# Mixture-of-experts block after cross-attention: expert tiles run in two phases, routing of the last batches placed between tiles

## The reference

```python
x = x + xattn(_layernorm(x), ctx_1024, mask, mask, Wq, Wkv, Wc)      # 16 heads of 8, softmax over 128 keys
logits = xf @ router_w.T                       # xf = layernorm(x), 4096 tokens, 8 experts
top_vals, top_idx = top_k(logits, 2); probs = softmax(top_vals)
for e in range(8):
    w = sum(where(top_idx == e, probs, 0))
    h = gelu(xf @ w1[e].T + b1[e])             # 128 -> 512
    out += w[:, None] * (h @ w2[e].T + b2[e])  # 512 -> 128
x = x + out
```

## Time and profile before

| | us |
|---|---|
| median of 3 runs | 504.89 (502.22 to 506.77) |
| the profiled execution, own time | 509.84 |
| its span | 507.7 |
| TensorE busy | 368.2 (73%) |
| VectorE busy | 281.1 (55%) |
| ScalarE busy | 230.5 (45%) |
| GpSimd busy | 224.6 (44%) |
| mean granted clock of TensorE | 0.84 |

### The profile page before, as it was taken

One profiled execution on the slowest core, in us unless ns is written; L12 is line 12 of the kernel. 1 busy time (PEld: TensorE's weight loads), 2 busy tenths in 40 slices (PEclk: granted clock), 3 DMA queues, 4 the chain that ended last, 5 costly groups with the idle time before them and its releaser, 6 DMA issues.

```text
span 507.7 us, 12389 instructions
## 1 busy us (share of the span) xinstructions
PE 368.2 (73%) x3715; PEld 285.6 (56%) x3715; DVE 281.1 (55%) x883; ACT 230.5 (45%) x536; POOL 224.6 (44%) x316
## 2 busy tenths in 40 slices
PE   2548889797979878585596400899898999998900
PEld 1133556464646545363364300899797998887900
DVE  7167998779666766554343762344343444443426
ACT  1314677667364654433354100466454665554500
POOL 7883422312370724334607471255453555444520
PEclk9999998879786798775767555899998999999965
DMA  4795345635242332010101023555565655565358
GB/s 125 176 254 156 98 119 108 151 85 139 79 123 77 103 96 71 26 40 29 43 5 38 23 68 96 162 168 182 158 181 161 180 174 171 159 184 167 95 163 334
DMA packets 57119, 63.00 MB, mean 124 GB/s; under 512 B 14109, under 2 KB 40116, under 8 KB 56896
## 3 DMA queue, kind: packets, MB, share of 16 engines
q1 hardware_dynamic: 51584, 53.22, 37.9%
q0 software_dynamic: 4320, 8.47, 4.9%
q10 hardware_dynamic: 1152, 0.53, 0.4%
HBM read 37.65 MB, written 11.88 MB: 98 GB/s over the span
## 4 chain that ended last, share of the span: by engine, by line
PE 40%; DVE 14%; SPq 13%; issue 9%; DMA 9%; another core or an unknown queue 7%; ACT 5%; ACTq 0%; POOLq 0%; POOL 0%; DVEq 0%
PE smax L1117 9%; PE sexp L1126 8%; DVE shift L1186 5%; PE tail L950 5%; PE smax L906 5%; DMA stacks<-dispatch_d 4%; PE feed L985 3%; SPq L409 2%; SPq L493 2%; SPq L486 2%; SPq L494 2%; PE feed L897 2%; ACT probs L752 2%; SPq L487 2%
## 5 line engine op out<-in xcount | busy, mean ns | idle before, releaser
L1186 DVE TENSOR_REDUCE shift<-smax 128x4 f32<-128x512 f32 x128 | 85.9, 683 | 68.3 <-PE smax L906 41.2
L752 ACT ACTIVATE probs<-sexp 128x512 f32<-128x512 f32 x128 | 73.9, 593 | 41.6 <-PE sexp L914 29.5
L632 POOL DMA_INDIRECT dispatch_d<-rows_out,row_i x64 | 63.0, 984 | 64.1 <-DVE row_i L1338 47.5
L681 POOL DMA_INDIRECT result_d<-y_out,stacks x71 | 70.8, 997 | 38.4 <-issue 36.4
L1557 DVE TENSOR_TENSOR probs<-smax,b_cols 128x512 f32<-128x512 f32 x71 | 49.1, 691 | 68.3 <-PE smax L1117 66.4
L1117 PE MATMUL smax<-probs,w_ring 128*128 128x128 f32 x568 | 81.7, 289 | 3.8 <-ACT probs L857 1.7
L1126 PE MATMUL sexp<-w_sb,probs 128*128 x568 | 79.0, 283 | 1.0 <-ACT probs L861 1.0
L1117 PEld LDWEIGHTS smax<-probs,w_ring 128*128 128x128 f32 x568 | 71.7, 198 | 11.6 <-issue 10.3
L906 PE MATMUL smax<-stacks 64*128 64x128 bf16 x512 | 59.5, 250 | 23.6 <-DVE shift L1186 10.5
L1126 PEld LDWEIGHTS sexp<-w_sb,probs 128*128 128x128 f32 x568 | 70.5, 195 | 2.6 <-issue 1.4
L906 PEld LDWEIGHTS smax<-stacks 64*128 64x128 bf16 x512 | 34.6, 107 | 54.4 <-issue 22.2
(11 more groups left out here) (191 smaller groups left out, 528.6 us busy)
## 6 DMA issues: line engine op xcount, KB each, us to landing
w_ring<-w_t_dram SPq DMA_DIRECT2D x71, 256.0 KB
stacks<-kpart SPq DMA_DIRECT2D x48, 128.0 KB
stacks<-qpart SPq DMA_DIRECT2D x48, 128.0 KB
stacks<-dispatch_d SPq DMA_DIRECT2D x71, 65.0 KB
stacks<-result_d SPq DMA_DIRECT2D x16, 256.0 KB, 5.4
ctx<-ctx_t_dram SPq DMA_DIRECT2D x8, 256.0 KB, 3.2
w_sb<-w_t_dram SPq DMA_DIRECT2D x8, 256.0 KB
out_dram<-xs SPq DMA_DIRECT2D x8, 256.0 KB, 5.9
```

Of the source, the lines that this page charges most:

```text
L632: nc.gpsimd.indirect_dma_start(out=dispatch_d, out_offset=bass.IndirectOffsetOnAxis(ap=row_i[r % RR][:, k, b:b + 1], axis=0), in_=rows_out ...
L681: nc.gpsimd.indirect_dma_start(out=result_d, out_offset=bass.IndirectOffsetOnAxis(ap=xg[r][:, D + 1:D + 2].bitcast(U32), axis=0), in_=y_ou ...
L752: nc.scalar.activation(dst, sexp[hp][:], ACT.Exp).then_inc(exp_done, 1)
L1186: nc.vector.tensor_reduce(shift4[n % 2][:, hp, 0, 4 * m:4 * m + 4], smax[hp][:], AX.X, ALU.max, negate=True).then_inc(max_taken, 1)
```

## The change

Rounds become eight of four batches. The 71 tiles are cut in two phases. `SPLIT = 6` rounds (24 batches, 6144 rows) are counted as soon as round 5 is ranked; each expert's rows of these batches fill whole tiles, and 40 (`FIRST`) such full tiles exist for any routing. A short table (18 steps, of which three in slot 34 and fifteen in slot 35) describes them, and tiles 0 to 39 start on it. The rest of round 6, round 7, the counts of all rows and the table of the 31 other tiles (32 steps more) are put between the tiles on every engine: on VectorE `between(t)`, on TensorE and ScalarE `if t == ...`, on GpSimd `SEND_TILE`. The second table works with 24 segments (8 experts by three stretches: whole tiles of the first phase, the others of the first 24 batches, those of the last 8).

Sends in the slots follow `SEND_COUNT`, two or three per slot, and from the second of a slot on each waits for a maximum or an exponential of that slot (`pace`). The pad rows are all stored by SyncE, one before each of tiles 26 to 33. The result rows of the first 24 batches all come from tiles below 55: ScalarE loads them from tile 60 on, VectorE adds a group after each of tiles 63 to 68, and SyncE stores these six groups after its last tile load. Two groups are left for the tail.

```diff
-ROUNDS = (0, 4, 8, 12, 16, 20, 24, 28, 31, 32)
+ROUNDS = (0, 4, 8, 12, 16, 20, 24, 28, 32)
-SEND_AT = (17, 21, 25, 28, 30, 34)
-SEND2_AT = (19, 23, 27, 29, 31, 35)
+SEND_COUNT = {18: ((0, 2),), 19: ((0, 2),), 20: ((0, 2),), 21: ((0, 2),),
...
+              32: ((4, 3),), 33: ((4, 3),), 34: ((4, 1),), 35: ((5, 4),), 36: ((5, 4),)}
+SPLIT = 6
+FIRST_ROWS = SPLIT * GB * SEQ * TOPK
+FIRST = (FIRST_ROWS - EXPERTS * (P - 1)) // P
+OLD_TILES = FIRST_ROWS // P + EXPERTS - 1
+PAD_TILE = 26
+SEND_TILE = {4: (6, 0), 5: (6, 1), 6: (6, 2), 8: (6, 3), 9: (6, 4), 10: (6, 5), 12: (6, 6), 13: (6, 7),
+             16: (7, 0), 17: (7, 1), 18: (7, 2), 20: (7, 3), 21: (7, 4), 22: (7, 5), 24: (7, 6), 25: (7, 7)}
+FOUND_TILE = 60
+ADD_TILE = 63
 # SyncE
-            sp.wait_ge(table_steps, PADS_STEP)
-            for e in range(0, EXPERTS, 2):
...
-            sp.wait_ge(table_steps, TABLE_STEPS)
+            sp.wait_ge(table_steps, FIRST_STEPS)
             for t in range(AHEAD):
                 load_w1(t, t)
-            for r in range(ROUND - RR, ROUND):
+            for r in range(SPLIT - RR, SPLIT):
                 rows_gone(sp, r)
-            sp.wait_ge(pads_sent, 16 * EXPERTS)
-            sp.wait_ge(idle_rows_stored, 16)
...
             for t in range(AHEAD, TILES):
+                if t == PAD_TILE:
+                    sp.wait_ge(table_steps, PADS_STEP)
+                if PAD_TILE <= t < PAD_TILE + EXPERTS:
+                    store_pad(t - PAD_TILE)
+                if t == FIRST:
+                    sp.wait_ge(table_steps, TABLE_STEPS)
                 load_w1(t, t % WRING)
+                if t == FIRST:
+                    for r in range(SPLIT, ROUND):
+                        rows_gone(sp, r)
+                    sp.wait_ge(pads_sent, 16 * EXPERTS)
+                    sp.wait_ge(idle_rows_stored, 16)
                 load_tile(t, t % TRING, t >= TRING)
+            for g in range(SPLIT):
+                sp.wait_ge(found_added, 2 * (g + 1))
+                sp.dma_start(out[:, part, :], xs[:, part, :]).then_inc(out_stored, 16)
+            tiles_stored(sp, TILES)
-            for g in range(GROUPS):
+            for g in range(SPLIT, GROUPS):
 # GpSimd
+            def pace(s, u):
+                if s < BATCH:
+                    pool.wait_ge(max_taken, UNITS * s + u)
+                elif s - LAG < BATCH:
+                    pool.wait_ge(exp_done, UNITS * (s - LAG) + u)
+                n = 0
+                for r, count in SEND_COUNT.get(s, ()):
+                    if sent[r] == 0:
+                        send_ready(r)
+                    for _ in range(count):
+                        n += 1
+                        if n > 1:
+                            pace(s, n)
+                        send_row(r, sent[r])
+                        sent[r] += 1
...
             for t in range(TILES):
+                r, n = SEND_TILE.get(t, (0, 0))
+                if r:
+                    if n == 0:
+                        send_ready(r)
+                    send_row(r, n)
                 store_tile(t, t % TRING, t == 0)
 # ScalarE, in the tile loop
+                if t == 1:
+                    share_ratio(6)
+                if t == 6:
+                    copy_normed(7)
+                if t == 11:
+                    share_ratio(7)
+                if t == FOUND_TILE:
+                    tiles_stored(act, OLD_TILES)
+                if FOUND_TILE <= t < FOUND_TILE + SPLIT:
+                    g = t - FOUND_TILE
+                    for k in range(TOPK):
+                        act.dma_start(found[k][:, part, :], found_d[k, :, part, :]).then_inc(found_loaded[g], 16)
 # TensorE
-            pe.wait_ge(table_steps, TABLE_STEPS)
+            pe.wait_ge(resid_done, BATCH)
+            pe.wait_ge(table_steps, FIRST_STEPS)
...
+                if t == 3:
+                    rank(6)
+                if t == 5:
+                    turn_rows(7)
+                if t == 7:
+                    project_router(7)
+                if t == 13:
+                    rank(7)
+                if t == 15:
+                    count_rows(7)
 # VectorE
+            def first_table():
+                last = run_sum(EXPERTS, (1, 2, 4))
+                link(nc.vector.tensor_scalar(seg_step[:, 0:EXPERTS], seg_tiles[:, 0:EXPERTS], -float(P), float(REGION),
+                                             ALU.mult, ALU.add))
+                at = slice(0, FIRST)
+                mark_passed(0, FIRST, EXPERTS, last)
...
+                if s == 34:
+                    first_counts()
+                if s == 35:
+                    first_table()
+            def between(t):
...
+                if t == 16:
+                    last_counts()
+                if t == 17:
+                    segments()
+                if t == 18:
+                    segment_steps()
+                if t == 19:
+                    later_passed()
+                if t == 20:
+                    later_starts()
+                if t == 21:
+                    later_experts()
+                if ADD_TILE <= t < ADD_TILE + SPLIT:
+                    add_found(t - ADD_TILE)
```

More of the change, by code:

```diff
@@ L215, in xattn_ffn @@
         heads_ps = heads[:, 0:2 * SEQ].rearrange("p (h c) -> p h c", c=VW)
[L216 to L217 removed]
+        total_ps = feed[:, 2 * GB * EXPERTS:2 * GB * EXPERTS + EXPERTS]
+        route_bank = [heads if r == ROUND - 1 else feed for r in range(ROUND)]
         logits_ps = [bank[:, 0:GB * EXPERTS] for bank in route_bank]
```

338 lines of the change are left out of this document (194 added, 144 removed), and 2 rows, old and new, of the table SEND_COUNT.

## The result

| | before | after |
|---|---|---|
| median of the runs, us | 505.83 (502.22 to 506.9, 4 runs) | 475.02 (467.66 to 477.57, 4 runs) |
| ratio, 95% interval | | 0.932 [0.918, 0.946] |
| profiled execution, its span, us | 509.84, 507.7 | 474.17, 472.1 |
| first tile load (start) | 314.00 | 262.02 |
| first to last tile load | 159.4 | 184.8 |

The changed kernel is 6.8% faster.

What follows compares the result with a forecast made beforehand. Bounds: attention's unpartnered waits, a serial handover, SyncE's pace late in the tiles, the tail. 507.7 - 25 - 20 + 12 + 3 - 8.5 = 469.2 us span, 467 in median terms; own range 454 to 480, with rivals 441 to 490.

Steps and rivals of the forecast that it cites:

- C: Tile stage: pads on SyncE, routing links and table switches lengthen it, GpSimd's delay stays hidden; +12 us.
- A: Handover: tile 0 no longer waits for the last eight batches, first tile load at 289 instead of 314.00; -25 us.
- B: Attention: thinner, paced row sends remove waits without a partner; -20 us (-33 to 0).
- D: Late tiles: six output groups loaded and added between tiles, with some loads late; +3 us (0 to +10).
- E: Tail: only four loads, four additions and two stores stay; -8.5 us (-10 to -5).
- one that was to show it wrong: Tile stage: tiles 4 to 26 taking over 2.7 us each with unpartnered waits among them would refute the forecast.
- Rival (2): Attention: the count of sends costs, not their density, so thinner sends gain 0; 486 us, chance 0.17.
- Rival (3): Handover: round 5's burst of eight holds TensorE's signals, first tile load at 305, early start gains 9; 483 us, chance 0.11.
- rival (4): Tiles 4 to 26: sends closer than 2.1 us hold TensorE, 1.2 us for each of 43, +52; 526 us, chance 0.04.

Runs made afterwards that it cites:

- x7: Kernel before with the changed kernel's table of sends for the first six rounds and its waits between them, nothing else: 481.10 us, ratio 0.953.
- x8: Changed kernel with loads, additions and stores of the first six output groups back behind the last tile: 474.77 us, ratio 0.941.
- x5: Changed kernel with the first six rounds' sends in bursts of four at twelve attention slots, without waits between sends: 494.55 us, ratio 0.969.
- x2: Changed kernel with its 16 tile-stage row sends in four blocks of four, at tiles 6, 9, 18 and 21: 471.22 us, ratio 0.935.
- x11: Changed kernel with its 16 tile-stage row sends in blocks of four behind the routing, at tiles 27, 29, 31 and 33: 473.55 us, ratio 0.940.
- x3: Changed kernel with the last two rounds' ratios computed by Gelu instead of Exp, changing their mixing shares: 468.15 us, ratio 0.935.
- x4: Changed kernel with the eight pad rows of tiles 26 to 33 stored by ScalarE instead of SyncE: 470.80 us, ratio 0.941.

## Why the prediction was right, and where it was not

The forecast was 467 us in a range of 441 to 490; the changed kernel takes 475.02. That the sum came within 3 us is partly luck: C missed by 13.4 us, and A, B, D and E together by 10.5 the other way. By the forecast's own list of signs two missed for the good (the first tile load is 52 us earlier, not 20 to 45; the end takes 11.4 us, not 13 to 16), two for the bad (the idle stretch is 16 us, not under 10; the tile loads span 184.8 us, not 165 to 175), and one that was to show it wrong came: tiles 3 to 25 take 3.25 us each, with waits without a partner among them.

| term | forecast | measured, us |
|---|---|---|
| A, early start | -25 | -26.7, from round 5's row numbers to the first tile load (45.5 before, 18.9 after) |
| B, sends in attention | -20 | -25.3 up to these row numbers; -19.9 by x7, which has it alone |
| C, tile stage | +12 | +25.4 |
| D, between tiles | +3 | +2.1 against before; 6.3 by x8 |
| E, tail | -8.5 | -11.1 against before; -11.8 by x8 |
| sum | -38.5 | -35.6 |

**Part B held**, as a cause and in size. Bursts of sends cost the attention stage some 18 us, pacing gives them back, and x5 and x7 show it in both directions, with the waits behind TensorE's products going the same way. That the burst itself holds the signal is the reading of these waits, and not every burst does it: beside the eight sends of round 5 the product was taken at once (252.21 above). Rival (2), by which the number of sends costs and not their spacing, is out for attention, as all five kernels send the same rows there. The other 5 us up to round 5's row numbers (248.2 in x7, 243.1 in the changed kernel) go with what else the reorder took out of attention's end; that was not tried apart.

**Part A held.** Of its steps, the sends began 5.8 us behind the row numbers (forecast 3.5) and ended 15.7 behind them (13.6), the first tile load stood 3.2 behind their end (3.1) and 18.9 behind the row numbers. The forecast had 20.5 there (289 - 268.47), since it let the last residual decide; that came 1.6 us before the end of the sends. The 15 links of the short table in slot 35 stand between 250.4 and 254.6, 4.2 us (4 to 7). Rival (3), by which this burst holds TensorE's signals, did not come. Unseen was that the burst itself, eight sends of round 5, would be the last thing before the tiles: they end at 258.8, the table at 254.6.

**Part C is the step that failed**: "It falls up to 11 us behind; a tile load reuses a buffer of 12 tiles earlier, which has about 8 tiles (17 us) of slack, so nobody waits." I costed the 16 row sends by what they do to GpSimd, whose delay is indeed hidden, and put their effect on TensorE's signals at nothing, because single stores every 2.1 us showed none. The sum by terms, from gate to gate of tiles 0 and 70 (159.6 us before, 186.7 after): sends 16 x 1.17 = 18.7 (forecast 0, or 19 by rival (4)'s price for each of the 16), links on VectorE with the rest of the routing work, its 23 matmuls too, 7.7 (5), table switches and ratios 3.6 (4), pads 0 (8.9), tiles 35 to 70 and the first ones +1.6. One wait of 3 to 4 us at tile 28 of the kernel before (5.3 us for that tile), which the forecast did not see, is for a tile load's data; x2, with no send in tiles 25 to 35, does not have it, and that takes 4.5 off. The pads cost nothing; SyncE stood waiting again and again in tiles 4 to 25, which is likely why. Links and tables, which the forecast laid beside the pads (11 us, of which it kept 3), stand by themselves at 11.3, nearly its 8.9 + 3; what was missed is the sends, 18.7 us.

Rival (4), sends that hold TensorE's signals, came nearest in kind but not in extent: by it all 43 sends and stores of tiles 4 to 26 would cost 1.2 us. About the price of the 16 is what the stage lost; stores one per tile stay free, stores in a row do not (x11 near tile 52). The forecast's sign against this rival, single stores every 2.1 us, said nothing of rows of three.

**Table loads.** The Trainium skill (ScalarE: Activation LUTs, What ACT_TABLE_LOAD costs) puts a change of table set at about 2.66 us; here four loads took 1.28 us each and x3 shows 2.2 us on the path for all four, so the trace's row was the better price, more than half of its 5.1 us was hidden, and the 10.6 us of the page's figure do not show.

**Parts D and E** were both too small, by about 3 us in x8's terms, with opposite signs; the net, -5.5, is what was forecast.

## What to carry to other kernels

In this kernel a row of indirect DMAs that GpSimd issues has a second price beside GpSimd's own time: VectorE and ScalarE take TensorE's products late, by 1 to 9 us, in many of these rows. Where the loop has slack, let each send wait for a step of TensorE's readers instead of issuing several in a row; where TensorE is the bound and a store stands in every iteration, count each further send at its full issue time or more (1.0 to 1.4 us here) and move it, if at all, to a stage that has slack. And cost a moved instruction on every engine that waits for a signal beside it, not only on its own engine and in the buffers.

## What was not expected of the hardware

- Most late signals end with the row of issues. TensorE's results are taken 0.2 us behind the end of GpSimd's last issue in the earlier trace rows (233.04 to 233.25), 1.0 at tile 25 and 1.3 in x2. VectorE's own short operations, 0.22 us apart, ran undisturbed beside eight sends (250.4 to 257.1 us). What in the chip holds the signals stays open, and so does why the burst of eight at 248.98 to 258.8 left no reader of TensorE waiting, where beside eight sends in slot 29 ScalarE waited 8.6 us.
- The same attention code, up to TensorE's matmuls for the maxima of batch 31, took 212.8 to 222.8 us in the profiled executions of the ten versions that do not differ there. It goes with TensorE's granted clock between 100 and 150 us: 0.93 to 1.00 in the three that took under 215, 0.80 to 0.88 in the seven that took over 217. The stretch in the changed kernel and in x4:

```profile
100.00:150.00 50.00, 43.46 (x599) 29.76 (x595) 38.45 (x134) 30.97 (x73) 14.89 (x20) 0.85 0.46 121
```

```profile
100.00:150.00 50.00, 41.83 (x634) 28.74 (x634) 43.15 (x144) 33.93 (x80) 19.12 (x24) 0.97 0.48 131
```

  The stretch got 634 matmuls done at 0.97 and 599 at 0.85. So some 9 us of a span go with the clock, whichever of the two is the cause; the tile stage, 182.0 to 188.6 in all versions that have its 16 sends, varied far less, and effects under 10 us could only be read there. The kernel before had 0.83 in that stretch, x7 0.85.
